# Two-layer attention on 8 images: one block of scores alternating with maxima, then one run of all values

## The reference

```python
h = group_norm(x, groups=32) * w + b          # 64 channels, 1024 tokens an image
q, k, v = h @ Wq + bq, h @ Wk + bk, h @ Wv + bv
scores = einsum('bnc,bmc->bnm', q, k) / 8     # 1024 x 1024 an image
attn = softmax(scores, axis=-1)
x = x + (attn @ v) @ Wo + bo
```

## Time and profile before

| what | value |
|---|---|
| median of 3 runs | 186.3 us (185.76 to 186.8) |
| profiled execution, its own time | 186.09 us |
| span of the profiled execution | 184.3 us |
| PE busy | 177.0 us (96%) |
| DVE busy | 132.4 us (72%) |
| POOL busy | 121.4 us (66%) |
| ACT busy | 100.3 us (54%) |

### The profile page before, as it was taken

How to read it: one execution, slowest core, us unless ns; L and a number is a source line. 1 busy time by engine, 2 the same in 40 slices (tenths; PEclk the granted TensorE clock), 3 DMA queues, 4 the chain that set the end, 5 groups by cost and what they waited for, 6 DMA issues and landing times.

```text
span 184.3 us, 3436 instructions
## 1 busy us (share of the span) xinstructions
PE 177.0 (96%) x1295; PEld 96.2 (52%) x1295; DVE 132.4 (72%) x200; ACT 100.3 (54%) x137; POOL 121.4 (66%) x79
## 2 busy tenths in 40 slices
PE   7988899999999999999999999999999999999993
PEld 3445545545535655455535655555535555456671
DVE  2789987679867686859676785769675586484743
ACT  4289367616656376446666476426656554466500
POOL 3265016996799929997699949996799939705000
PEclk9999999999999999999999999999999999999998
DMA  5534100500025000420024001600025101010111
GB/s 152 190 78 107 43 5 0 114 4 2 0 50 124 3 0 18 114 44 0 4 70 102 0 0 31 146 4 0 1 66 111 57 0 46 16 57 16 44 57 57
DMA packets 8896, 8.90 MB, mean 48 GB/s; under 512 B 1656, under 2 KB 5936, under 8 KB 8880
## 3 DMA queue, kind: packets, MB, share of 16 engines
q1 hardware_dynamic: 7648, 7.90, 17.5%
q10 hardware_dynamic: 1232, 0.79, 1.5%
HBM read 1.58 MB, written 1.05 MB: 14 GB/s over the span
## 4 chain that ended last, share of the span: by engine, by line
PE 90%; DVE 8%; issue 1%; POOL 0%; ACT 0%; DVEq 0%; POOLq 0%
PE ps_attn L878 28%; PE ps_max L808 10%; PE ps_scores L846 8%; PE ps_scores L862 7%; PE ps_scores L850 7%; DVE part_max L588 7%; PE ps_scores L848 7%; PE ps_scores L787 4%; PE ps_scores L774 3%; PE ps_misc L795 3%; PE ps_misc L893 2%; PE ps_attn L885 2%; PE ps_misc L885 1%; PE ps_misc L822 1%; PE ps_scores L849 1%; PE ps_scores L863 1%
## 5 line engine op out<-in xcount | busy, mean ns | idle before, releaser
L315 POOL TENSOR_TENSOR prob_sum<-prob_sum,probs 128x1024 f32<-128x1024 f32 x41 | 97.6, 2379 | 29.0 <-ACT probs L442 16.8
L588 DVE TENSOR_REDUCE part_max<-ps_max 128x2 f32<-128x1024 f32 x60 | 73.4, 1223 | 31.3 <-PE ps_max L809 30.9
L442 ACT ACTIVATE probs<-ps_scores 128x1024 f32<-128x1024 f32 x62 | 61.0, 1026 | 46.1 <-PE ps_scores L863 45.4
L878 PE MATMUL ps_attn<-probs,vals 128*64 128x512 f32 x224 | 54.5, 605 | 0.0
L878 PEld LDWEIGHTS ps_attn<-probs,vals 128*64 128x64 f32 x224 | 13.5, 136 | 26.5 <-issue 17.9
L862 PE MATMUL ps_scores<-q_row,ones_r 64*128 64x512 f32 x62 | 24.5, 396 | 0.5 <-ACT q_row L424 0.5
L863 PE MATMUL ps_scores<-q_row,ones_r 64*128 64x512 f32 x62 | 24.6, 396 | 0.0
L808 PE MATMUL ps_max<-back,front 64*128 64x512 f32 x31 | 14.0, 450 | 1.4 <-DVE part_max L588 1.4
L808 PE MATMUL ps_max<-cross,front 64*128 64x512 f32 x29 | 14.7, 505 | 0.3 <-DVE part_max L588 0.3
L809 PE MATMUL ps_max<-cross,back 64*128 64x512 f32 x29 | 14.6, 505 | 0.0
L809 PE MATMUL ps_max<-front,back 64*128 64x512 f32 x31 | 14.0, 451 | 0.0
(11 more groups left out here) (157 smaller groups left out, 365.8 us busy)
## 6 DMA issues: line engine op xcount, KB each, us to landing
cross<-front SPq DMA_DIRECT2D x16, 128.0 KB, 2.3
cross<-back SPq DMA_DIRECT2D x16, 128.0 KB, 2.3
rden<-block_rden SPq DMA_DIRECT2D x46, 32.0 KB, 1.9
xs<-x_dram SPq DMA_DIRECT2D x4, 256.0 KB, 4.6
out_dram<-xs SPq DMA_DIRECT2D x3, 256.0 KB, 2.0
rden<-block_rden ACTq DMA_DIRECT2D x10, 32.0 KB, 1.9
q_row<-max_rows SPq DMA_DIRECT2D x14, 2.0 KB
layer<-layers_dram SPq DMA_DIRECT2D x1, 194.5 KB, 2.6
```

The costliest lines, as they stand in the source:

```text
L315: pool.tensor_tensor(total[:, :], total[:, :], probs[t][:, :], ALU.add).then_inc(added, 1)
L442: act.activation(probs[t][:, :], scores_buffer(u, t)[:, :], ACT.Exp, scale=SCALE).then_inc(exp_done, 1)
L588: dve.tensor_reduce(part_max[u % 2][:, at:at + 2 * JS + 1:2 * JS], ps[:, :].rearrange("p (g n) -> p g n", g=2), AX.X, ALU.max, negate=True ...
L878: mm = pe.matmul(ps_attn[half * C:(half + 1) * C, :], v, probs[t][:, cols], start=(t == 0), stop=(t == TILES - 1))
```

## The change

The unit on PE becomes: eight blocks of scores alternating with the eight maxima of `w+1`, then `denominators(w-1)`, values 0 to 5, `turn_max(w+1)`, `project(w+2)`, values 6, `project_v(w+2)`, values 7. The maxima alternate between `ps_max` and `ps_both`, which joins the banks of `ps_attn` and `ps_misc`; the last takes `ps_scores[0]`, and projections from unit 2 on go to `ps_scores[1]`. On ACT all eight exponentials come first, then `apply_norm(w+2)`, the two copies of `spread_rden(w-1)`, `stage_max(w+1)`, `bias_x`, the high parts, `copy_v`, `copy_attn(w)`. On DVE `first_add(w)` follows part 2, and statistics, reciprocal, `affine` and low parts follow part 7. On POOL `root(w+2)` moves behind `add(w,4)`. On SP `place_rows(w+1)` moves ahead of `spread_rden(w-1)` and the swaps. In unit 7 all eight blocks of scores come before the values; `denominators(6)` follows values 0 and 1 and writes to `ps_max`; DVE takes `reciprocal(6)` behind `add_late(4)`.

```diff
-        ps_attn = psum("ps_attn", [P, HALF])
-        ps_misc = psum("ps_misc", [P, HALF])
+        ps_both = psum("ps_both", [P, N])
+        ps_attn = ps_both[:, 0:HALF]
+        ps_misc = ps_both[:, HALF:N]
+        def projected(unit):
+            return ps_scores[0] if unit < HEAD else ps_scores[1]
+        def max_buffer(m):
+            return (ps_max, ps_both, ps_max, ps_both, ps_max, ps_both, ps_max, ps_scores[0])[m]
...
             for w in range(UNITS):
+                if w + 1 < UNITS:
+                    place_rows(w + 1)
                 if w:
                     spread_rden(w - 1)
                 if w + 2 < UNITS:
                     swap_hi(w + 2)
                     swap_lo(w + 2)
-                if w + 1 < UNITS:
-                    place_rows(w + 1)
...
-            root(2)
             for w in range(UNITS):
-                if 3 <= w + 2 < UNITS:
-                    root(w + 2)
                 for t in range(2, 2 + pool_adds(w)):
                     add(w, t)
+                    if t == 4 and w + 2 < UNITS:
+                        root(w + 2)
                     if t == 5 and 0 < w < LAST - 1:
                         finish(w - 1)
...
+                for t in range(TILES):
+                    exp(w, t)
                 if prep:
                     apply_norm(w + 2)
                 if 1 < w < LAST:
                     spread_rden(w - 1)
-                if 0 < w < LAST:
+                if w < LAST:
                     stage_max(w + 1)
                 if prep:
                     bias_x(w + 2)
+                    high_front(w + 2)
+                    high_back(w + 2)
+                    copy_v(w + 2)
+                if w < LAST:
+                    copy_attn(w)
...
+            for w in range(LAST):
                 prep = w + 2 < UNITS
+                part(w + 1, 0)
+                part(w + 1, 1)
+                part(w + 1, 2)
+                first_add(w)
+                for m in range(3, TILES):
+                    part(w + 1, m)
+                join(w + 1, neg_max[:, :])
                 if prep:
                     own_stats(w + 2)
                     share_stats(w + 2)
                     join_stats(w + 2)
+                if w:
+                    reciprocal(w - 1)
                 if prep:
                     affine(w + 2)
                     low_front(w + 2)
                     low_back(w + 2)
+            pair_tail(LAST - 1)
             finish_tail(LAST - 2)
-            pair_tail(LAST - 1)
             add_tail(LAST - 1)
             first_add(LAST)
+            add_late(3)
+            add_late(4)
             reciprocal(LAST - 1)
...
+            def next_max(w, m):
+                u = w + 1
+                if m == 0:
+                    pe.wait_ge(max_done, TILES * u if w else TILES - 1)
+                elif m == 1:
+                    pe.wait_ge(max_staged, u)
+                    pe.wait_ge(v_copied, min(w + 2, UNITS))
+                    if w:
+                        pe.wait_ge(attn_copied, w)
+                    if w > 1:
+                        pe.wait_ge(rden_done, w - 1)
+                elif m < TILES - 1:
+                    pe.wait_ge(max_done, TILES * u + m - 1)
+                else:
+                    pe.wait_ge(exp_done, TILES * w + TILES - 1)
+                partial_max(u, m, max_buffer(m))
...
+            for w in range(LAST):
                 prep = w + 2 < UNITS
+                if w:
+                    next_max(w, 0)
+                    scores(w, 0)
+                for t in range(1, TILES - 3):
+                    next_max(w, t)
+                    scores(w, t)
+                scores(w, 5)
+                next_max(w, 5)
+                scores(w, 6)
+                next_max(w, 6)
+                scores(w, 7)
+                next_max(w, 7)
+                pe.wait_ge(max_done, TILES * (w + 1) + 6)
+                if w:
+                    denominators(w - 1)
                 values(w, 0)
                 values(w, 1)
                 values(w, 2)
                 values(w, 3)
                 values(w, 4)
                 values(w, 5)
+                if w:
+                    pe.wait_ge(rden_done, w)
+                turn_max(w + 1)
+                if prep:
+                    project(w + 2)
+                values(w, 6)
                 if prep:
                     pe.wait_ge(max_staged, w + 2)
                     project_v(w + 2)
+                values(w, 7)
...
             def denominators_last():
+                pe.wait_ge(rden_done, LAST)
                 pe.wait_ge(late_added, TILES - 4)
```

More of the change, by code:

```diff
@@ L582, in low_back, with part @@
                                          op0=ALU.add, op1=ALU.subtract).then_inc(back_lo, 1)
-            def part(u, m, ps=ps_max):
+            def part(u, m, ps=None):
+                ps = ps if ps is not None else max_buffer(m)
                 crossed, j = divmod(m, JS)
@@ L696, in _ @@
             join_second()
[L697 to L734, removed]
-                prep = w + 2 < UNITS
+            for w in range(LAST):
+                prep = w + 2 < UNITS
+                part(w + 1, 0)
[5 more added lines that the diff above has]
+                join(w + 1, neg_max[:, :])
@@ L751, in _ @@
-                part(w + 1, 7)
-                join(w + 1, neg_max[:, :])
-                if prep:
                     low_front(w + 2)
                     low_back(w + 2)
-                    part(w + 2, 0)
-                    part(w + 2, 1)
+            pair_tail(LAST - 1)
             finish_tail(LAST - 2)
-            pair_tail(LAST - 1)
             add_tail(LAST - 1)
             first_add(LAST)
+            add_late(3)
+            add_late(4)
             reciprocal(LAST - 1)
-            for t in range(3, TILES - 1):
-                add_late(t)
+            add_late(5)
@@ L765, in _ @@
+            add_late(6)
             finish_tail(LAST - 1)
@@ L832, in scores_main @@
                     pe.wait_ge(*low_count(back_lo, head_back_lo, u))
+                    if u:
+                        pe.wait_ge(max_done, TILES * (u + 1))
+                if t == 1 and 0 < u < LAST:
+                    pe.wait_ge(front_lo, u)
+                    pe.wait_ge(back_lo, u)
                 g = TILES * u + t
@@ L979, in _ @@
             scores_row(0, 0)
-            max_after(TILES + 1, 1, 1)
-            scores(0, 1)
-            max_after(TILES + 2, 1, 2)
-            scores(0, 2)
-            scores(0, 3)
-            max_after(TILES + 3, 1, 3)
-            values(0, 0)
-            values(0, 1)
-            max_after(TILES + 4, 1, 4)
-            scores(0, 4)
-            scores(0, 5)
-            max_after(TILES + 5, 1, 5)
-            pe.wait_ge(exp_done, 5)
-            project(2)
-            values(0, 2)
-            values(0, 3)
@@ L996, in _ @@
-            max_after(TILES + 6, 1, 6)
-            pe.wait_ge(front_lo, 1)
-            pe.wait_ge(back_lo, 1)
-            scores(0, 6)
-            scores(0, 7)
-            max_after(TILES + 7, 1, 7)
-            values(0, 4)
-            values(0, 5)
-            turn_max(1)
-            max_after(2 * TILES, 2, 0)
-            pe.wait_ge(max_staged, 2)
-            project_v(2)
-            max_after(2 * TILES + 1, 2, 1)
-            scores(1, 0)
-            scores(1, 1)
-            max_after(2 * TILES + 2, 2, 2)
@@ L1094, in _ @@
                     project_v(w + 2)
-            scores(LAST, 0)
-            scores(LAST, 1)
-            scores(LAST, 2)
-            values(LAST - 1, 6)
-            values(LAST - 1, 7)
-            pe.wait_ge(max_staged, UNITS)
-            denominators(LAST - 1)
-            scores(LAST, 3)
-            scores(LAST, 4)
-            scores(LAST, 5)
-            pe.wait_ge(rden_done, LAST)
+                values(w, 7)
+            for t in range(TILES):
+                scores(LAST, t)
+            pe.wait_ge(max_staged, UNITS)
             values(LAST, 0)
             values(LAST, 1)
-            scores(LAST, 6)
-            scores(LAST, 7)
+            denominators(LAST - 1)
             values(LAST, 2)
```

124 lines of the change are left out of this document (16 added, 108 removed).

## The result

The changed kernel takes 213.2 us (median of 4 runs) against 186.5 before: the ratio is 1.142, 95% interval 1.135 to 1.149. The profiled execution took 212.74 for a span of 210.9.

The account below looks back on a forecast made before the run. PE bounded the kernel before; after, a closed loop of 15.45 + 0.5 + 1.6 + 6.5 = 24.05 us a unit against PE's 19.9. Four turns plus start and tail gave a span of 207, so 209 us, range 204 to 215.

Parts of the forecast that it names:

- Bound and saving: PE bounds the kernel before; values in one run save 0.6 us of form changes, PE's unit 20.5 to 19.9 us.
- The loop: From one finish to the next, POOL to DVE to ACT to SP to POOL: 24.05 us, a lower bound of the unit.
- POOL's 15.45: POOL's loop term: finish 2.60, two additions 4.86, three more 7.43, root 0.56 us.
- ACT's 1.6: ACT's loop term: stage_max starts 1.3 us after apply_norm's start, behind two reciprocal copies, and takes 0.27.
- SP's 6.5: SP's loop term: two row copies 1.38 us, six copies at 0.64 each, the last landing 1.9 later.
- The first addition on DVE: DVE's addition after part 2 takes 1.21 us and is caught up where blocks 4 and 5 stand together.
- The sum: Whole run: finish(0) at 64.5, four turns of 24.05, last reciprocal at 199.1 to 200.7, end taken as 207 us.
- rival C: PE's clock falls to 1.2 GHz in the tail and at the body's waits: 212 to 217 us; chance 0.17.
- The waits named: PE loses 0.25 us at maximum 4 (swaps), 1.0 before denominators, 2.9 before project.
- rival D: Later swaps make maximum 4 wait longer, lost in PE's later waits; changes no number under 3.9 us.
- Rival A: Loop does not close if copies cost no issue time; gain goes in the tail, 185 to 186.6 us; chance 0.05.
- Rival B: Shorter loop through PE alone if root were served early: 20.9 us a unit, 196 us; chance 0.08.

Follow-up runs that it names:

- experiment 9: Changed kernel with SP issuing the copies of the reciprocals ahead of the row copies and POOL doing finish(w-1) behind add(w,7): 188.1 us, ratio 1.010.
- experiment 1: Changed kernel with SP issuing the six copies of the reciprocals ahead of the two row copies: 195.0 us, ratio 1.039.
- experiment 2: Changed kernel with root(w+2) on POOL behind add(w,2) instead of add(w,4): 200.6 us, ratio 1.077.
- 3: Changed kernel with finish(w-1) on POOL behind add(w,7) instead of add(w,5): 194.9 us, ratio 1.048.
- experiment 8: Changed kernel with four copies of the reciprocals a unit instead of eight from unit 1 on: 198.3 us, ratio 1.067.
- Experiment 5: Changed kernel with DVE's first addition covering 8 of 1024 columns in units 2 to 6, all waits kept: 210.0 us, ratio 1.131.
- 4: Changed kernel with six extra matmuls on PE ahead of project in units 2 to 5: 212.95 us, ratio 1.143.
- 10: As experiment 9, with denominators(6) behind unit 7's fourth score block, add_tail ahead of finish_tail(5), reciprocal(6) after the first addition: 181.9 us, ratio 0.978.
- experiment 6: Changed kernel with ACT issuing its two copies of the reciprocals behind stage_max instead of ahead of it: 213.4 us, ratio 1.146.
- 7: Changed kernel with ACT's two copies behind stage_max and six extra matmuls on PE ahead of project: 210.6 us, ratio 1.132.

## Why the prediction was right

**Bound and saving.** Right: PE alone bounded before, and the one run of values saves what was said. The units without a loop came to 19.8 us (experiment 9) for 19.9 predicted.

**The loop.** Right, link by link, and shown: cut at SP's order, at root's place or at `finish`'s place it opens or shortens (1, 2, 3), four issues less shorten it by 2.6 (8). Predicted 24.05 us, measured 24.7, 24.9, 24.9 and 25.5. The term that was mis-sized is POOL's 15.45, from `finish` to the end of `root`. It measured 16.2 (88.53 to 104.74). The rows of before showed each operation at the price it has when DVE is not in the way, because `first_add` then came while POOL was idle or in `root`; the change laid it on POOL's `finish` and additions. Experiment 5 took 0.8 us of it back. The turn of 25.5 has 0.4 us more of issue time on SP (4.23 instead of 3.81) besides. The other terms held: DVE's 0.5 was 0.44, ACT's 1.6 was 1.66, SP's 6.5 was 6.59. One row was misread, and nothing hangs on it: in the kernel before, SP issues the copies (91.33) 7.6 us before POOL starts `finish` (98.88), not six.

**The first addition on DVE.** "the addition after part 2 (1.21) is caught up where blocks 4 and 5 stand together": it took up to 2.63, and maximum 5 waited 0.58 us in unit 3. In the changed kernel the loop covers that on PE; in experiment 1 it took 3.1, and maximum 5 waited 1.08 us in every other unit. That the longer turns there (22.4 and 22.9 instead of 19.8), and with them my miss, come from it fits experiment 9, where it took 1.22 and these turns were gone; other waits moved in that run too. The Trainium skill (SBUF — State Buffer, Who interferes with whom) says that DVE and GpSimd share a pair of ports under an exclusive lock, and that a DVE instruction with two inputs in SBUF contends with a GpSimd instruction that reads SBUF. The rows agree: the 8-column addition took 1.77 us behind POOL, 0.16 without.

**The sum.** Predicted 207 for the span, measured 210.9. `finish(0)` came at 63.8 (64.5 predicted), the four turns took 100.0 us instead of 96.2, and from `finish(4)` to the last reciprocal it was 40.1 instead of 39.2, with DVE's first addition on POOL's `finish` there as well (2.26 us). -0.7, +3.8 and +0.9 make 4.0, and 0.1 less behind the last reciprocal (7.0 for 7.1) leaves the 3.9 between 207 and 210.9. The measured 213.2 is above the 205 to 212 that the prediction gave to its own mechanism. It is inside the stated range because that reached to 215 for rival C, the fallen clock, and the clock is not what took the time (4): so far this was luck. What took it, two engines in each other's way, was not foreseen.

**The waits named.** PE waits 2.85 us for the norm in three units, 2.9 predicted, and 1.11 in unit 3, where it comes late: from the start of `project` to the next unit took 6.9 us at the low clock in unit 2 and 3.8 in unit 3. Before `denominators` it waits up to 1.0 us for POOL, 1.0 predicted. The swaps cost 1.36, 0, 1.40 and 0.23 us in units 2 to 5, 0.25 predicted: in unit 2 eight copies stand ahead of them on SP instead of six, and in unit 4 one swap's issue took 1.41 us instead of 0.59. None of these waits is a term of the 24.90, as rival D had it.

**Rival A** needed issues without a price; experiment 8 puts them at 0.64 us each. But its second half was right: with the loop open (9) the kernel is not faster than before, and it is once the reciprocal of unit 6 and its sums stand earlier (10). **Rival B**'s 20.9 is the leg through PE: 21.4 to 21.7 in three of four turns of experiment 2. **Rival C**: the granted clock did fall to 1.2 GHz, behind all three of PE's waits of 2.85 us and in the tail, but holding it up alone gave nothing (4); it counted once the loop was 0.6 us shorter (6, 7). The sentence of the Trainium skill that this rival cites stands in that page (TensorE: Matmul & The Clock Gate) under What's actually happening, and these falls agree with it. What follows the last wait ran at full speed (0.0 instead of the 2.7 us of the rival); the slow stretch (197.84 on) lay before it, where PE had time. In experiment 9 what follows the last wait did run partly at half speed, for 1.3 us.

**Open.** Why single copies are now and then issued or landed 0.4 to 1.3 us late, which goes with turns of 25.3 to 25.7 in several runs; no run isolates it.

## What to carry to other kernels

Write down, for every queue that a step is moved past, who waits for what is behind it, and follow the waits until they leave the engines or close: a closed loop's length is a lower bound of the period, whatever share of the time its engines are busy (POOL was at 60% in the changed kernel). And do it for each order afresh: the same move on SP closed one loop in the new order and a longer one in the old. A gain in the loop body has then to be followed into the last unit, where it was lost once more until the sums and the reciprocal of unit 6 were moved ahead.

## What the runs showed of the hardware

- A DVE addition of two tiles in memory and a POOL operation wait for one another: the addition took 1.22 us alone and up to 3.12 behind POOL (experiment 1), and POOL's 1.29 became 1.92 or 2.14 behind DVE (changed kernel). DVE's reductions from the banks kept their 1.21 to 1.23 beside POOL.
- Issues of the copies of reciprocals (32 KB, landing 1.9 us later) stood 0.64 us apart on SP and took 0.55 to 0.62 us on ACT. Four fewer made a turn 2.6 us shorter (8), and two moved behind a small activation let it start 0.65 us earlier (6).
- PE's granted clock fell from 2.4 to 1.2 GHz at all three waits of 2.85 us in the changed kernel (in units 2 and 5 before PE went on, so that a pair of `project` took 1.0 us instead of 0.53; in unit 4 about 0.9 us after it), and at two of three such waits in experiment 6. It was back at 2.4 GHz 3 to 6.5 us after PE went on. With these waits filled by matmuls it stayed at 2.4 GHz in the body (4).
